# Softmax sums from the exp instruction to VectorE, chains one pair later, token-shift products on ScalarE

## The chip, the cores and the metric

One Trainium2 chip, all 8 of its cores, one launch. Each core works on one half of one of the four sequences and needs nothing from the others while it runs; cores of a pair read the same 4096 tokens in opposite order of halves. The metric is the device time in microseconds (us) of the slowest core, as a median over runs.

## The reference, cut to what matters

```python
x = x + attn(layernorm(x))            # x: (4, 4096, 1024) f32
x = x + ffn(layernorm(x))

def attn(z):                          # Wq, Wk, Wv: 1024 x 64
    q, k, v = z @ Wq, z @ Wk, z @ Wv
    att = softmax(einsum('bid,bkd->bik', q, k), axis=1)   # over the QUERIES i, for each key k
    return tile(att @ v, (1, 1, 16))  # 64 columns, repeated 16 times

def ffn(z):                           # W_r, W_k, W_v: 1024 x 1024
    z_prev = z shifted by one token (zeros first)
    xr = mu_r * z + (1 - mu_r) * z_prev
    xk = mu_k * z + (1 - mu_k) * z_prev
    r = sigmoid(xr @ W_r.T)
    return r * (square(relu(xk @ W_k.T)) @ W_v.T)
```

The softmax normalises each key over all 4096 queries. So with keys on the partitions its sum is one sum per partition over 4096 elements, and 1/sum can be multiplied into the key's row of v.

## The kernel before, in words

Every core normalises all 4096 tokens, computes q, k and v for them, runs the attention of all 4096 keys against all 4096 queries (columns of its own half are kept, see below), and runs the second layernorm and the feed-forward part for its own 2048 tokens. One program is written as a row of blocks per engine; each engine takes its blocks in program order, and counted semaphores tie them: SM counts TensorE's groups, SV VectorE's instructions, SS ScalarE's, the others count DMAs by 16.

The stages, in order:

- **A, layernorm** (L318 to L427): 32 tiles of 128 tokens, written to DRAM as bf16 and brought back transposed as `zT`.
- **C, projections** (L434 to L489): q and k, each written twice (`qrep`, `krep`: the same 64 rows on both halves of the partitions), then v, which goes through DRAM (`vdram`) and comes back as `v_sb` in 32 transposing DMAs, one after the other, on SyncE's queue (L485). TensorE's scores for the first pair wait only for the projections.
- **D, attention** (L515 to L608). Keys come in tiles `kt` of 128, 32 of them, handled as 16 pairs `q` = (2q, 2q+1). For each pair the queries are cut into 4 strips `s` of 1024. TensorE writes the scores of one strip of one key tile into one of three PSUM units of 128x1024 (two matmuls of 512 columns, L544); the even tile uses the upper 64 rows of the array, the odd one the lower 64. A unit is free again when the exp three places back has read it (`d_exp(ktp_, sp_)`, L539). VectorE takes a maximum of every fourth of the first 512 scores of the tile (`reduce_max` to `negm`, L569). ScalarE takes exp of each strip with bias `negm`, writes bf16 into `p_sb[kt % 4]` (4 buffers of 128x4096) and, by `accum_out`, the strip's sum into `ellp` (L604). VectorE then runs what is called **the chain** here, per key tile: add the four strip sums (`ell`, L575), reciprocal (`rell`, L579), scale the tile's 64 columns of v (`vs_sb`, L582), copy one column of p (`xp_sb`, L585). TensorE adds the tile's part of the output, v times p, over four strips of 512 query columns (4 matmuls, L525; they run two at a time, on the two column halves of the array), in `dpool[:, 0:1024]`.
- **E** (L620 to L679): that sum is copied out (L623), turned to token order, and one extra token, the one before the core's half, is treated by a row of tiny steps.
- **F, second layernorm** (L697 to L819), result to DRAM as `z1dram`, and back transposed as `z1T` (8 tiles by 128 channels x 2080 tokens). The first halves of the token range are 8 DMAs issued by ScalarE (L827), the second halves 8 more, each waiting for the one before (L836), issued by ScalarE too.
- **H, token shift** (L855 to L879): per channel tile `ct` VectorE computes `xr[ct]` in two instructions (L864: `z1T * mu`; L867: `z1T shifted * (1 - mu) + that`), in place, and after all eight `xr` the same for `xk` (L873, L876).
- **I, J, K**: r (L897, sigmoid L910), the squared relu (L937, L953, L962), the last product with the sum and the stores (L994, L1039 to L1049). TensorE begins I after the last `xr` (`h_xr_all`); the first sigmoid waits until all of H is done (`SV_H`, L907), as `r_sb` lies where `z1T` was.

What sets the order around the change is the order on each engine in stage D:

- TensorE, pair q (from q = 2): the output matmuls of tiles 2q-4 and 2q-3, each behind `d_vsc` of its tile (the scaled v), and only behind them the 16 score matmuls of pair q.
- VectorE, pair q, before: maximum of 2q, maximum of 2q+1, chain of 2q, chain of 2q+1. A chain waits for the last exp of its tile (`d_exp(kt, 3)`).
- ScalarE, pair q: eight exps, strip by strip, even and odd tile by turns; the first of each tile waits for its maximum, for the row `ell` of two tiles back, and for the output matmuls of four tiles back.

Of the kernel before, what the change touches and what calls it, by code (L numbers as in the profile page):

```python
# [26 lines left out]
def build_program(debug=False):  # L27
# [33 lines left out]
    with ctx:  # L61
# [6 lines left out]
        mu = e(nc.sbuf_tensor("mu", [128, 16], F32))  # L68
# [137 lines left out]
        SM_D0, SS_D0, SV_D0 = SM_C, SS_A, SV_C  # L206
# [9 lines left out]
        def d_outmm(t):  # L216
            q = t // 2
            if q <= 13:
                return SM_D0 + d_P(q + 2) - 4 * (1 - (t % 2))
            return SM_D0 + 368 + 8 * (q - 14) + 4 * (t % 2 + 1)  # L220
        d_exp = lambda kt, s: SS_D0 + 8 * (kt // 2) + 2 * s + (kt % 2) + 1
        d_max = lambda kt: SV_D0 + 10 * (kt // 2) + (kt % 2) + 1
        d_ellsum = lambda kt: SV_D0 + 10 * (kt // 2) + 3 + 4 * (kt % 2)
        d_recip = lambda kt: SV_D0 + 10 * (kt // 2) + 4 + 4 * (kt % 2)
        d_vsc = lambda kt: SV_D0 + 10 * (kt // 2) + 5 + 4 * (kt % 2)
        d_xp = lambda kt: SV_D0 + 10 * (kt // 2) + 6 + 4 * (kt % 2)
        SM_D = SM_D0 + 384
        SS_D = SS_D0 + 128
        SV_D = SV_D0 + 160
        e_evac = SV_D + 2  # L230
        e_tpmm = lambda b: SM_D + b + 1
        e_oxmm = SM_D + 16 + KT
# [2 lines left out]
        SM_E = e_oxmm  # L235
# [31 lines left out]
        F_CNT, SV_Floop = plan_ln_af2(TOWN, SV_TAIL)  # L267
# [3 lines left out]
        SS_F = SS_TAIL + 20  # L271
# [6 lines left out]
        sd_zero2 = SD_E0 + 96  # L278
        SD_F = sd_zero2
        szt_g_hi = lambda ct: 16 * (ct + 1)  # L280
        SV_H0 = SV_F + 1
        h_xr_all = SV_H0 + 16
        SV_H = SV_H0 + 32
        SH_ALL = 0
        SM_I0, SS_I0 = SM_E, SS_F
        i_mm = lambda t: SM_I0 + t + 1
        i_sig = lambda t: SS_I0 + t + 1
        SM_I = SM_I0 + 16
# [272 lines left out]

        @block.vector
        def _(v):
            for q in range(KT // 2):
                for a in range(2):
                    kt = 2 * q + a
                    u0 = d_eidx(kt, 0) % 3
                    v.wait_ge(SM, d_smm(kt, 1))
                    v.reduce_max(negm[:, kt:kt + 1],  # L569
                                 units[u0][:, 0:512:4],  # L570
                                 axis=AX.X, negate=True).then_inc(SV, 1)
                for a in range(2):
                    kt = 2 * q + a
                    v.wait_ge(SS, d_exp(kt, 3))
                    v.reduce_sum(ell[:, kt:kt + 1],  # L575
                                 ellp[:, 4 * (kt % 2):4 * (kt % 2) + 4],
                                 axis=AX.X).then_inc(SV, 1)
                    v.wait_ge(SV, d_ellsum(kt))
                    v.reciprocal(rell[:, kt:kt + 1], ell[:, kt:kt + 1]).then_inc(SV, 1)  # L579
                    v.wait_ge(SV, d_recip(kt))  # L580
                    v.wait_ge(SVT, 16 * (kt + 2))
                    v.tensor_scalar(vs_sb[:, kt * D:(kt + 1) * D],  # L582
                                    v_sb[:, kt * D:(kt + 1) * D],
                                    rell[:, kt:kt + 1], None, ALU.mult).then_inc(SV, 1)
                    v.tensor_copy(xp_sb[:, kt:kt + 1],  # L585
                                  p_sb[kt % 4][:, 4095:4096]).then_inc(SV, 1)

        @block.scalar
        def _(sc):
            for q in range(KT // 2):  # L590
                for s in range(4):
                    for a in range(2):
                        kt = 2 * q + a
                        u = d_eidx(kt, s) % 3
                        if s == 0:
                            if kt == 0:
                                sc.wait_ge(SVT, 16)
                            sc.wait_ge(SV, d_max(kt))
                            if kt >= 2:
                                sc.wait_ge(SV, d_ellsum(kt - 2))  # L600
                            if kt >= 4:
                                sc.wait_ge(SM, d_outmm(kt - 4))
                        sc.wait_ge(SM, d_smm(kt, 2 * s + 1))
                        sc.activation(p_sb[kt % 4][:, s * 1024:(s + 1) * 1024],  # L604
                                      units[u][:, :], AF.Exp,
                                      bias=negm[:, kt:kt + 1],
                                      accum_out=ellp[:, 4 * (kt % 2) + s:
                                                     4 * (kt % 2) + s + 1]).then_inc(SS, 1)  # L608

        @block.gpsimd  # L610
        def _(g):
# [209 lines left out]
        @block.scalar  # L821
        def _(sc):
            sc.wait_ge(SD, sd_zero1)
            for s in range(8):
                sc.wait_ge(ZSs[s], 16)
            for ctn in range(CT):
                sc.dma_start(out=z1T[ctn][:, 0:1040],  # L827
                             in_=z1dram[0:1040, ctn * 128:(ctn + 1) * 128],
                             transpose=True).then_inc(SG_LO, 16)
            sc.wait_ge(SD, sd_zero2)  # L830
            for s in range(8):
                sc.wait_ge(ZSs[s], 32)
            sc.wait_ge(SG_LO, 128)
            for ctn in range(CT):
                sc.wait_ge(SG_HI, 16 * ctn)
                sc.dma_start(out=z1T[ctn][:, 1040:2080],  # L836
                             in_=z1dram[1040:2080, ctn * 128:(ctn + 1) * 128],
                             transpose=True).then_inc(SG_HI, 16)

# [12 lines left out]
        xr = opens(xr_cm)  # L852
        dbuf = zst[:, 0:2048]

        @block.vector  # L855
        def _(v):
            v.wait_ge(SS, f_square(15))
            v.scalar_tensor_tensor(mu1m[:, :], mu[:, :], -1.0, onec[:, :],
                                   ALU.mult, ALU.add).then_inc(SV, 1)
            v.wait_ge(SV, SV_H0)  # L860
            for ct in range(CT):
                v.wait_ge(SG_HI, szt_g_hi(ct))
                v.wait_ge(SV, SV_H0 + 2 * ct)
                v.tensor_scalar(xr[ct][:, :], z1T[ct][:, 16:2064],  # L864
                                mu[:, ct:ct + 1], None, ALU.mult).then_inc(SV, 1)
                v.wait_ge(SV, SV_H0 + 2 * ct + 1)
                v.scalar_tensor_tensor(xr[ct][:, :], z1T[ct][:, 15:2063],  # L867
                                       mu1m[:, ct:ct + 1],
                                       xr[ct][:, :], ALU.mult,
                                       ALU.add).then_inc(SV, 1)  # L870
            for ct in range(CT):
                v.wait_ge(SV, SV_H0 + 16 + 2 * ct)
                v.tensor_scalar(xk[ct][:, :], z1T[ct][:, 16:2064],  # L873
                                mu[:, 8 + ct:9 + ct], None, ALU.mult).then_inc(SV, 1)
                v.wait_ge(SV, SV_H0 + 16 + 2 * ct + 1)
                v.scalar_tensor_tensor(xk[ct][:, :], z1T[ct][:, 15:2063],  # L876
                                       mu1m[:, 8 + ct:9 + ct],
                                       xk[ct][:, :], ALU.mult,
                                       ALU.add).then_inc(SV, 1)  # L879
# [231 lines left out]
```

## Time and profile before

| | us |
|---|---|
| median of 2 runs | 744.12 |
| the two runs | 739.31, 748.92 |
| the profiled execution, its own time | 739.37 |
| span of its slowest core (core 7), from which all rows are | 737.8 |
| spans of the 8 cores | 724.1 to 737.8 |
| VectorE, ScalarE, TensorE matmuls busy | 308.8, 244.0, 364.9 |

The span runs from the first to the last instruction of the core; 1.6 us lie around it. In rows, a time at the start of a line is us from the start of the span, and the number behind it the duration in us (of several instructions, where the line ends in x2 or more, from the first start to the last end or busy together). PE is TensorE (PEld its weight loads), DVE VectorE, ACT ScalarE, POOL GpSimd, SP SyncE; a name with q is that engine's queue of instructions and DMA issues. Square brackets hold the idle time of the engine before the instruction, and what ended it.

### The profile page before, as it was taken

To read this page: it belongs to the slowest core of one execution; us is meant where nothing else is said; L and a number is where in the kernel's file an instruction comes from. 1 tells how busy PE (TensorE), PEld (TensorE's weight loads), DVE (VectorE), ACT (ScalarE), POOL (GpSimd) and SP (SyncE) were. 2 spreads that over 40 slices of the span, in tenths; PEclk is the share of its full clock that TensorE was granted. 3 is DMA by queue.
4 is the path that set the end of the run, shared out by engine and by line. 5 is a ranking of instruction groups with operands and counts; after the bars stand their busy time and mean duration, and the time that the engine had idled before them with its cause. 6 is when DMAs were issued, how large, how long until landed. Compare 5 with 4: busy or idle time off the path is not lost.

```text
span 737.8 us, 5703 instructions; the slowest of 8 cores (724.1 to 737.8 us)
## 1 busy us (share of the span) xinstructions
PE 364.9 (49%) x1392; PEld 125.0 (17%) x1392; DVE 308.8 (42%) x531; ACT 244.0 (33%) x420; POOL 25.4 (3%) x45
## 2 busy tenths in 40 slices
PE   0004000006967888888872000000509999998984
PEld 0001000002421111111111000000104444443431
DVE  4702608147721101111131598808980002226987
ACT  3204013050028898889850233200012233330000
POOL 2000000000000030000000011000000000001110
PEclk9999655556985555555555555555659999999998
DMA  9966985837010099900000045284100000008664
GB/s 237 293 140 81 309 126 190 229 93 161 11 30 8 6 128 160 277 20 0 1 0 1 5 169 172 85 162 78 21 0 0 1 1 1 0 1 274 229 234 175
DMA packets 79044, 75.82 MB, mean 103 GB/s; under 512 B 59427, under 2 KB 59443, under 8 KB 78948
## 3 DMA queue, kind: packets, MB, share of 16 engines
q1 hardware_dynamic: 17124, 38.88, 15.9%
q0 software_dynamic: 10944, 23.93, 14.2%
q10 hardware_dynamic: 50944, 12.65, 10.7%
q8 instruction: 12, 0.20, 0.1%
q14 instruction: 20, 0.16, 0.1%
HBM read 47.79 MB, written 21.56 MB: 94 GB/s over the span
## 4 chain that ended last, share of the span: by engine, by line
DMA 27%; PE 22%; DVE 21%; issue 13%; ACTq 7%; ACT 6%; SPq 2%; DVEq 1%
DMA v_sb<-vdram 10%; PE ktp L937 7%; PE rps L897 7%; ACTq L362 5%; DMA zdram<-zst 5%; DMA z1T<-z1dram 4%; ACT p_sb L604 4%; DMA y_out<-x2b 3%; DVE x1b L735 3%; DMA xst<-x_in 3%; DVE xk L876 3%; PE dpool L544 2%; DVE tmp L1043 2%; DVE sums L415 2%; DVE tmp L1039 2%
## 5 line engine op out<-in xcount | busy, mean ns | idle before, releaser
L604 ACT ACTIVATE p_sb<-dpool,negm 128x1024 bf16<-128x1024 f32 x128 | 140.6, 1125 | 21.9 <-DVE negm L569 21.9
L897 PE MATMUL rps<-wrT,xr 128*128 128x512 bf16 x256 | 59.4, 397 | 150.4 <-DVE xr L867 131.0
L544 PE MATMUL dpool<-qrep,krep 64*128 64x512 bf16 x256 | 110.8, 605 | 32.7 <-ACT p_sb L604 27.3
L443 PE MATMUL qk<-zT,wqk 128*128 128x512 bf16 x64 | 18.5, 441 | 163.6 <-DVE qrep L474 99.1
L348 ACT ACTIVATE zst<-xst 128x1024 bf16<-128x1024 f32 x32 | 33.8, 1056 | 104.2 <-issue 91.7
L994 PE MATMUL ops<-wvT,kaT 128*128 128x512 bf16 x256 | 58.4, 387 | 8.2 <-DVE tmp L1039 6.6
L575 DVE TENSOR_REDUCE ell<-ellp 128x1 f32<-128x4 f32 x32 | 5.0, 157 | 134.7 <-ACT p_sb L604 134.7
L897 PEld LDWEIGHTS rps<-wrT,xr 128*128 128x128 bf16 x256 | 25.8, 101 | 183.6 <-issue 156.1
L937 PE MATMUL ktp<-xk,wkT 128*128 128x512 bf16 x256 | 55.6, 379 | 1.7 <-ACT r_sb L910 1.3
L962 DVE TENSOR_TENSOR kaT<-kaT 128x512 bf16<-128x512 bf16 x32 | 13.6, 425 | 97.6 <-ACT kaT L953 97.5
L415 DVE TENSOR_REDUCE sums<-xst 128x1 f32<-128x1024 f32 x32 | 37.3, 1211 | 11.8 <-DMA xst<-x_in 11.8
L544 PEld LDWEIGHTS dpool<-qrep,krep 64*128 64x128 bf16 x256 | 16.8, 105 | 125.0 <-issue 124.8
L372 DVE TENSOR_SCALAR smean<-sums,cconst 128x4 f32<-128x4 f32 x12 | 2.8, 229 | 81.5 <-ACT zst L348 80.1
L443 PEld LDWEIGHTS qk<-zT,wqk 128*128 128x128 bf16 x64 | 6.8, 108 | 173.0 <-issue 167.4
L994 PEld LDWEIGHTS ops<-wvT,kaT 128*128 128x128 bf16 x256 | 24.9, 99 | 41.7 <-issue 14.5
L953 ACT ACTIVATE kaT<-ktp 128x512 bf16<-128x512 f32 x32 | 19.0, 597 | 34.5 <-PE ktp L937 34.5
L937 PEld LDWEIGHTS ktp<-xk,wkT 128*128 128x128 bf16 x256 | 24.9, 98 | 32.3 <-issue 2.6
L812 ACT ACTIVATE zst<-x1b 128x1024 bf16<-128x1024 f32 x16 | 16.9, 1056 | 36.1 <-DVE x1b L735 36.1
L910 ACT ACTIVATE r_sb<-rps 128x1024 bf16<-128x1024 f32 x16 | 16.3, 1024 | 36.1 <-PE rps L897 36.1
L604 ACT ACTIVATION_READ_ACCUMULATOR p_sb<-dpool,negm 128x1 f32 x128 | 27.7, 217 | 0.0
L525 PE MATMUL dpool<-p_sb,v_sb 128*64 128x512 bf16 x112 | 26.9, 634 | 0.0
L910 ACT ACT_TABLE_LOAD x1 | 1.3, 1283 | 75.5 <-DVE xk L876 75.5
(82 smaller groups left out, 369.5 us busy)
## 6 DMA issues: line engine op xcount, KB each, us to landing
xst<-x_in SPq DMA_DIRECT2D x32, 512.0 KB, 9.0
xst<-x_in POOLq DMA_DIRECT2D x32, 512.0 KB, 6.7
zdram<-zst SPq DMA_DIRECT2D x32, 256.0 KB, 8.2
y_out<-x2b SPq DMA_DIRECT2D x16, 512.0 KB, 3.4
z1dram<-z1b SPq DMA_DIRECT2D x16, 256.0 KB, 2.9
wrT<-wrT_in POOLq DMA_DIRECT2D x1, 2048.0 KB, 19.2
wkT<-wkT_in POOLq DMA_DIRECT2D x1, 2048.0 KB, 31.2
wvT<-wvT_in POOLq DMA_DIRECT2D x1, 2048.0 KB, 44.2
```

Of the source, the lines that this page charges most:

```text
L348: sc.activation(zst[:, (i % 8) * C:(i % 8 + 1) * C], xst[:, (i % 8) * C:(i % 8 + 1) * C], AF.Square, accum_out=sumsq[:, i % 8:i % 8 + 1]). ...
L362: sc.dma_start(out=zT[ctn][:, qtr * 1024:(qtr + 1) * 1024], in_=zdram[qtr * 1024:(qtr + 1) * 1024, ctn * 128:(ctn + 1) * 128], transpose=T ...
L415: v.reduce_sum(sums[:, i % 8:i % 8 + 1], xst[:, (i % 8) * C:(i % 8 + 1) * C], axis=AX.X).then_inc(SV, 1)
L443: t.matmul(qk[buf][:, :], wqk[:, ct * 128:(ct + 1) * 128], zT[ct][:, nch * 512:(nch + 1) * 512], start=(ct == 0), stop=(ct == CT - 1), ski ...
L525: t.matmul(dpool[64 * half:64 * half + 64, (w % 2) * 512:(w % 2) * 512 + 512], vs_sb[:, tt_ * D:(tt_ + 1) * D], p_sb[tt_ % 4][:, w * 512:( ...
L544: t.matmul(units[u][:, cc * 512:(cc + 1) * 512], krep[64 * a:64 * (a + 1), kt * 128:(kt + 1) * 128], qrep[64 * a:64 * (a + 1), c * 512:(c ...
L604: sc.activation(p_sb[kt % 4][:, s * 1024:(s + 1) * 1024], units[u][:, :], AF.Exp, bias=negm[:, kt:kt + 1], accum_out=ellp[:, 4 * (kt % 2) + s:
L735: v.tensor_tensor(x1b[:, s8 * C:(s8 + 1) * C], xst[:, s8 * C:(s8 + 1) * C], bass.AP(out_tok, t_ * D, [[TOWN * D, 128], [0, 16], [1, D]]), ...
L876: v.scalar_tensor_tensor(xk[ct][:, :], z1T[ct][:, 15:2063], mu1m[:, 8 + ct:9 + ct], xk[ct][:, :], ALU.mult, ALU.add).then_inc(SV, 1)
L897: ins = t.matmul(r_ps[t_ % 2][:, hh * 512:(hh + 1) * 512], xr[ct][:, t_ * 128:(t_ + 1) * 128], wrT[:, ct * C + hh * 512:ct * C + (hh + 1) ...
L937: ins = t.matmul(kt_ps[ix % 2][:, :], wkT[:, ct * C + dt * 128:ct * C + (dt + 1) * 128], xk[ct][:, tc * 512:(tc + 1) * 512], start=(ct == ...
L994: ins = t.matmul(o_ps[t_ % 2][:, hh * 512:(hh + 1) * 512], kaT[dt][:, t_ * 128:(t_ + 1) * 128], wvT[:, dt * C + hh * 512:dt * C + (hh + 1) ...
```

## The change

Three parts.

1. **Softmax sums.** The exp (L604) has no `accum_out` any more. VectorE's `reduce_sum` in the chain reads the four strips themselves, 128x4096 bf16 of `p_sb[kt % 4]`, in place of the four numbers of `ellp`. ScalarE's wait for `ell` of two tiles back goes; for kt >= 4 a wait comes for `d_xp(kt - 4)`, the last instruction of the chain that reads the same buffer of p.
2. **Order on VectorE.** In pair q the two maxima come first, and then the chains of pair q-1, not of q; the chains of pair 15 follow at the end. TensorE's order is as it was.
3. **Token shift.** The two products `z1T * mu` of each channel tile go from VectorE to ScalarE (`Identity` with a scale per partition). VectorE keeps the second instruction of each. The 8 second-half transposes of `z1T` go from ScalarE's queue to SyncE's, with the same waits.

```diff
-        d_max = lambda kt: SV_D0 + 10 * (kt // 2) + (kt % 2) + 1
...
+        D_CNT = {}
+        _sv = SV_D0
+        for _q in range(16):
+            for _a in range(2):
+                _sv += 1
+                D_CNT[("max", 2 * _q + _a)] = _sv
+            if _q >= 1:
+                for _a in range(2):
+                    _kt = 2 * (_q - 1) + _a
+                    for _op in ("ellsum", "recip", "vsc", "xp"):
+                        _sv += 1
+                        D_CNT[(_op, _kt)] = _sv
...
         @block.vector
         def _(v):
+            def d_chain(v, kt):
+                v.wait_ge(SS, d_exp(kt, 3))
+                v.reduce_sum(ell[:, kt:kt + 1],
+                             p_sb[kt % 4][:, :],
+                             axis=AX.X).then_inc(SV, 1)
+                v.wait_ge(SV, d_ellsum(kt))
+                v.reciprocal(rell[:, kt:kt + 1], ell[:, kt:kt + 1]).then_inc(SV, 1)
+                v.wait_ge(SV, d_recip(kt))
+                v.wait_ge(SVT, 16 * (kt + 2))
+                v.tensor_scalar(vs_sb[:, kt * D:(kt + 1) * D],
+                                v_sb[:, kt * D:(kt + 1) * D],
+                                rell[:, kt:kt + 1], None, ALU.mult).then_inc(SV, 1)
+                v.tensor_copy(xp_sb[:, kt:kt + 1],
+                              p_sb[kt % 4][:, 4095:4096]).then_inc(SV, 1)
...
-                for a in range(2):
-                    kt = 2 * q + a
-                    v.wait_ge(SS, d_exp(kt, 3))
-                    v.reduce_sum(ell[:, kt:kt + 1],
-                                 ellp[:, 4 * (kt % 2):4 * (kt % 2) + 4],
-                                 axis=AX.X).then_inc(SV, 1)
...
+                if q >= 1:
+                    for a in range(2):
+                        d_chain(v, 2 * (q - 1) + a)
+            for a in range(2):
+                d_chain(v, 30 + a)
...
-                            if kt >= 2:
-                                sc.wait_ge(SV, d_ellsum(kt - 2))
                             if kt >= 4:
+                                sc.wait_ge(SV, d_xp(kt - 4))
                                 sc.wait_ge(SM, d_outmm(kt - 4))
...
-                                      bias=negm[:, kt:kt + 1],
-                                      accum_out=ellp[:, 4 * (kt % 2) + s:
-                                                     4 * (kt % 2) + s + 1]).then_inc(SS, 1)
+                                      bias=negm[:, kt:kt + 1]).then_inc(SS, 1)
...
-            sc.wait_ge(SD, sd_zero2)
+        @block.sync
+        def _(sy):
+            sy.wait_ge(SD, sd_zero2)
             for s in range(8):
-                sc.wait_ge(ZSs[s], 32)
-            sc.wait_ge(SG_LO, 128)
+                sy.wait_ge(ZSs[s], 32)
+            sy.wait_ge(SG_LO, 128)
             for ctn in range(CT):
-                sc.wait_ge(SG_HI, 16 * ctn)
-                sc.dma_start(out=z1T[ctn][:, 1040:2080],
+                sy.wait_ge(SG_HI, 16 * ctn)
+                sy.dma_start(out=z1T[ctn][:, 1040:2080],
...
+        @block.scalar
+        def _(sc):
+            sc.wait_ge(SV, F_CNT[("apply", 15)])
+            for ct in range(CT):
+                sc.wait_ge(SG_HI, szt_g_hi(ct))
+                sc.activation(xr[ct][:, :], z1T[ct][:, 16:2064], AF.Identity,
+                              bias=0.0, scale=mu[:, ct:ct + 1]).then_inc(SS, 1)
+            for ct in range(CT):
+                sc.activation(xk[ct][:, :], z1T[ct][:, 16:2064], AF.Identity,
+                              bias=0.0, scale=mu[:, 8 + ct:9 + ct]).then_inc(SS, 1)
...
             for ct in range(CT):
-                v.wait_ge(SG_HI, szt_g_hi(ct))
-                v.wait_ge(SV, SV_H0 + 2 * ct)
-                v.tensor_scalar(xr[ct][:, :], z1T[ct][:, 16:2064],
-                                mu[:, ct:ct + 1], None, ALU.mult).then_inc(SV, 1)
-                v.wait_ge(SV, SV_H0 + 2 * ct + 1)
+                v.wait_ge(SS, h_tsr(ct))
+                v.wait_ge(SV, SV_H0 + ct)
                 v.scalar_tensor_tensor(xr[ct][:, :], z1T[ct][:, 15:2063],
...
```

The semaphore counts of later stages follow (`SS_H` 16 more on ScalarE, `SV_H` 16 fewer on VectorE).

## Rows read from the trace of the kernel before

**Rows 1.** Busy by stretch: TensorE, weight loads, VectorE, ScalarE, GpSimd; granted clock, DMA share, GB/s
```profile
175.00:215.00 40.00, 36.23 (x162) 15.62 (x160) 22.91 (x35) 0.00 (x0) 0.00 (x0) 0.96 0.32 59
...
250.00:420.00 170.00, 118.03 (x362) 24.91 (x360) 32.77 (x159) 116.38 (x210) 6.89 (x11) 0.51 0.34 64
```

**Rows 2.** Timeline, one pair of key tiles in steady state, and its successor's first exp
```profile
337.55 1.92 PE L525 MATMUL dpool<-p_sb,v_sb 128*64 128x512 bf16 x8
...
339.40 1.88 PE L544 MATMUL dpool<-qrep,krep 64*128 64x512 bf16 x6
...
339.86 0.16 DVE L575 TENSOR_REDUCE ell<-ellp 128x1 f32<-128x4 f32 x1 [0.20 <-ACT p_sb L604]
...
340.46 0.24 DVE L582 TENSOR_SCALAR v_sb<-v_sb,rell 128x64 bf16<-128x64 bf16 x1 [0.18 <-DVE rell L579]
...
340.68 0.48 DVE L569 TENSOR_REDUCE negm<-dpool 128x1 f32<-128x128 f32 x2
341.22 1.11 ACT L604 ACTIVATE p_sb<-dpool,negm 128x1024 bf16<-128x1024 f32 x1 [1.47 <-DVE negm L569]
342.23 0.19 ACT L604 ACTIVATION_READ_ACCUMULATOR p_sb<-dpool,negm 128x1 f32 x1
342.33 1.11 ACT L604 ACTIVATE p_sb<-dpool,negm 128x1024 bf16<-128x1024 f32 x1
...
351.56 1.11 ACT L604 ACTIVATE p_sb<-dpool,negm 128x1024 bf16<-128x1024 f32 x1 [1.47 <-DVE negm L569]
```

**Rows 3.** Groups by line and shape: busy us, mean ns; idle before, releasers
```profile
L415 DVE TENSOR_REDUCE sums<-xst 128x1 f32<-128x1024 f32 x32 | 37.3, 1211 | 11.8 <-DMA xst<-x_in 11.8
...
L604 ACT ACTIVATION_READ_ACCUMULATOR p_sb<-dpool,negm 128x1 f32 x128 | 27.7, 217 | 0.0
...
L735 DVE TENSOR_TENSOR x1b<-xst,out_tok 128x1024 f32<-128x1024 f32 x16 | 19.4, 1213 | 0.0
...
L962 DVE TENSOR_TENSOR kaT<-kaT 128x512 bf16<-128x512 bf16 x32 | 13.6, 425 | 97.6 <-ACT kaT L953 97.5
...
L575 DVE TENSOR_REDUCE ell<-ellp 128x1 f32<-128x4 f32 x32 | 5.0, 157 | 134.7 <-ACT p_sb L604 134.7
```

**Rows 4.** Timeline, the last chain and the output matmuls behind it
```profile
381.83 0.24 DVE L582 TENSOR_SCALAR v_sb<-v_sb,rell 128x64 bf16<-128x64 bf16 x1 [0.18 <-DVE rell L579]
...
382.30 0.22 PEld L554 LDWEIGHTS dpool<-p_sb,v_sb 128*64 128x64 bf16 x4 [0.88 <-issue]
383.33 1.22 DVE L623 COPY out_sb<-dpool 64x1024 f32<-64x1024 f32 x1 [1.20 <-PE dpool L554]
```

**Rows 5.** Timeline, the first pair: scores, maxima, first exp
```profile
211.51 1.02 PE L544 MATMUL dpool<-qrep,krep 64*128 64x512 bf16 x6 [0.94 <-DVE p_sb L478]
212.21 0.49 DVE L569 TENSOR_REDUCE negm<-dpool 128x1 f32<-128x128 f32 x2 [0.84 <-PE dpool L544]
...
217.16 1.11 ACT L604 ACTIVATE p_sb<-dpool,negm 128x1024 bf16<-128x1024 f32 x1
```

**Rows 6.** Timeline, token shift: last two xr instructions, first and last xk, what follows
```profile
521.36 0.75 DVE L864 TENSOR_SCALAR xr<-z1T,mu 128x2048 bf16<-128x2048 bf16 x1 [0.39 <-DMA z1T<-z1dram]
522.22 2.35 DVE L867 SCALAR_TENSOR_TENSOR xr<-z1T,mu1m,xr 128x2048 bf16<-128x2048 bf16 x1
524.68 0.75 DVE L873 TENSOR_SCALAR xk<-z1T,mu 128x2048 bf16<-128x2048 bf16 x1
...
548.75 2.35 DVE L876 SCALAR_TENSOR_TENSOR xk<-z1T,mu1m,xk 128x2048 bf16<-128x2048 bf16 x1
551.24 1.28 ACT L910 ACT_TABLE_LOAD   x1 [75.47 <-DVE xk L876]
```

**Rows 7.** Groups of ScalarE by shape, for the price of a 2048-element product
```profile
L953 ACT ACTIVATE kaT<-ktp 128x512 bf16<-128x512 f32 x32 | 19.0, 597 | 34.5 <-PE ktp L937 34.5
...
L812 ACT ACTIVATE zst<-x1b 128x1024 bf16<-128x1024 f32 x16 | 16.9, 1056 | 36.1 <-DVE x1b L735 36.1
L910 ACT ACTIVATE r_sb<-rps 128x1024 bf16<-128x1024 f32 x16 | 16.3, 1024 | 36.1 <-PE rps L897 36.1
```

More of the change, by code:

```diff
@@ L221, in build_program @@
         d_exp = lambda kt, s: SS_D0 + 8 * (kt // 2) + 2 * s + (kt % 2) + 1
-        d_max = lambda kt: SV_D0 + 10 * (kt // 2) + (kt % 2) + 1
[L223 to L226, printed above, removed]
+        D_CNT = {}
[10 more added lines that the diff above has]
+                        D_CNT[(_op, _kt)] = _sv
+        for _a in range(2):
+            _kt = 30 + _a
+            for _op in ("ellsum", "recip", "vsc", "xp"):
+                _sv += 1
+                D_CNT[(_op, _kt)] = _sv
+        d_max = lambda kt: D_CNT[("max", kt)]
+        d_ellsum = lambda kt: D_CNT[("ellsum", kt)]
+        d_recip = lambda kt: D_CNT[("recip", kt)]
+        d_vsc = lambda kt: D_CNT[("vsc", kt)]
+        d_xp = lambda kt: D_CNT[("xp", kt)]
         SM_D = SM_D0 + 384
         SS_D = SS_D0 + 128
-        SV_D = SV_D0 + 160
+        SV_D = _sv
+        assert SV_D == SV_D0 + 160
         e_evac = SV_D + 2
@@ L280, in build_program @@
         szt_g_hi = lambda ct: 16 * (ct + 1)
+        SS_H0 = SS_F
+        h_tsr = lambda ct: SS_H0 + ct + 1
+        h_tsk = lambda ct: SS_H0 + 8 + ct + 1
+        SS_H = SS_H0 + 16
         SV_H0 = SV_F + 1
-        h_xr_all = SV_H0 + 16
-        SV_H = SV_H0 + 32
+        h_xr_all = SV_H0 + 8
+        SV_H = SV_H0 + 16
         SH_ALL = 0
-        SM_I0, SS_I0 = SM_E, SS_F
+        SM_I0, SS_I0 = SM_E, SS_H
         i_mm = lambda t: SM_I0 + t + 1
@@ L571, in _ @@
                                  axis=AX.X, negate=True).then_inc(SV, 1)
-                for a in range(2):
-                    kt = 2 * q + a
-                    v.wait_ge(SS, d_exp(kt, 3))
-                    v.reduce_sum(ell[:, kt:kt + 1],
-                                 ellp[:, 4 * (kt % 2):4 * (kt % 2) + 4],
-                                 axis=AX.X).then_inc(SV, 1)
[L578 to L586, printed above, removed]
+                if q >= 1:
[3 more added lines that the diff above has]
+                d_chain(v, 30 + a)
         @block.scalar
@@ L871, in _ @@
             for ct in range(CT):
[L872 to L875, printed above, removed]
+                v.wait_ge(SS, h_tsk(ct))
+                v.wait_ge(SV, SV_H0 + 8 + ct)
                 v.scalar_tensor_tensor(xk[ct][:, :], z1T[ct][:, 15:2063],
```

## The prediction

> **What bounds the kernel now.** I read the stretches first (busy time by stage), then the chain of waits, then the timeline of each place that the change touches, and last the groups of instructions by shape for prices. The stage that matters is the attention. From 250 to 420 us ScalarE is busy 116 of 170 us, VectorE 33, TensorE 118 at a granted clock of 0.51, its lower level of 1.2 GHz [rows 1]. One pair of key tiles takes 351.56 - 341.22 = 10.34 us [rows 2]: eight exps that start 1.09 to 1.11 us apart (8.8 us), and some 1.5 us in which ScalarE waits for the maximum of the next pair, which VectorE takes only after both chains of this pair. So ScalarE's exps set the pair, with a short turn over VectorE in between; VectorE is free for most of it. Sixteen pairs, from the first exp at 217.16 [rows 5] to the copy of the result at 383.33 [rows 4], are 166.2 us. The second place is the token shift, where VectorE works alone: its products and sums end at 548.75 + 2.35 = 551.1, and the first sigmoid's table load starts at 551.24 [rows 6]. TensorE stands still behind it.
>
> **Part 1: the exp without its sum.** The 128 accumulator reads cost 27.7 us of busy time [rows 3], but they overlap their neighbours: the read starts 1.01 us after its exp, and the next exp 0.10 us after the read [rows 2]. Without the read the next instruction can start at the same 1.01, so an exp saves 0.1 us, a pair 0.8 us: 8.1 us of exps. That would be about 13 us in all, if ScalarE still set the pair.
>
> **Part 2: the sum on VectorE.** The four-element sum (0.157 us, 32 times [rows 3]) becomes one over 4096 bf16. The trace has no such instruction. The same operation takes 1211 ns for 1024 elements and 157 for 4 [rows 3]: (1211 - 157) / 1020 = 1.033 ns an element, and 157 + 4092 x 1.033 = 4.39 us. Those inputs are f32. The other end: an elementwise bf16 operation takes 425 ns for 512, where an f32 one takes 1213 for 1024 [rows 3], so some bf16 work goes at twice the rate; a sum at that rate would take 157 + 4092 x 0.517 = 2.27 us. On the other hand `scalar_tensor_tensor` on bf16 needs 2.35 us for 2048 [rows 6], 1.15 ns an element, so bf16 alone speeds nothing up; at its rate the sum takes 4.71. I take 4.39, from the same operation, and keep 2.27 and 4.71 as ends.
>
> The Trainium skill has a rule for just this: VectorE: DVE Perf Modes, section "The perf-mode tier table", says that `tensor_reduce` has a program for one element a cycle only, in bf16 as in f32, while tensor_tensor goes twice as fast in bf16. No row of the kernel before shows a bf16 sum, so the trace neither confirms nor denies it. By this rule the sum stays at 4.39, by the tensor_tensor row it would be 2.27. The rule speaks against the change.
>
> **The chain.** In rows 2 the second chain starts its sum at 339.86; take off the sum's 0.16. From the sum's end to the end of the scaled v (340.46 + 0.24) is 0.68 us, to the start of the next VectorE instruction (340.68) 0.66. So a chain now takes 4.39 + 0.66 = 5.05 us, and 4.39 + 0.68 = 5.07 to its scaled v. Two of them are 10.1 us, against 8.1 us of exps: VectorE is the slower engine.
>
> **The order, and the loop that it closes.** The chains of pair q-1 now follow the maxima of pair q. TensorE was not reordered: before its scores for pair q it must do the output matmuls of tile 2q-3, which need that tile's scaled v. Before, that v was ready a pair earlier. Now it is made by VectorE directly ahead of the maximum of 2q. That maximum needs the scores of pair q, they stand in TensorE's queue behind those output matmuls, and these need the chain just ended. VectorE cannot run ahead, since its own next instruction is that maximum. So each pair goes round one closed loop:
>
> - from the scaled v of 2q-3 to the weight load of its output matmuls 0.23 us (381.83 + 0.24 = 382.07 to 382.30 [rows 4]);
> - 0.03 to the matmuls, and half of the 339.40 - 337.55 = 1.85 us that eight of them hold TensorE [rows 2]: 0.93;
> - the first two score matmuls, until VectorE starts its maximum. At a granted clock of 0.96 [rows 1] this was 212.21 - 211.51 = 0.70 us [rows 5]. Two 512-column matmuls are 0.43 us of it at 2.4 GHz and 0.86 at 1.2 GHz, where the attention runs: 1.13;
> - the second maximum waits for two more score matmuls. Six take 1.88 us [rows 2], so two take 0.63 where they overlap; then its own 0.24 (two are 0.48 [rows 2]);
> - the two chains of pair q-1, whose exps are long done: 5.05 + 5.07.
>
> The sum is 0.23 + 0.03 + 0.93 + 1.13 + 0.63 + 0.24 + 10.12 = 13.3 us a pair, against 10.34. ScalarE starts pair q's exps after the maxima, needs 8.1 us and then waits some 5 us. The new wait for `d_xp(kt - 4)` costs nothing, as the maximum of the same tile is later on VectorE; the saved 0.1 us per exp is worth nothing, as it lies in that wait.
>
> **The attention from end to end.** The first exp stays at 217.16. The sixth ends at 217.16 + 5 x 1.01 + 1.11 = 223.3, which frees the unit for the first scores of pair 1. The second unit comes free 1.0 later (224.3), and with 1.2 us for scores and signalling the second maximum starts at 225.5 and ends at 225.8. There the first sum starts. Fourteen rounds later (14 x 13.3 = 186.3) the chain of tile 28 starts, at 412.1; three chains and a last scaled v (3 x 5.05 + 5.07 = 20.2) end at 432.3, and the copy of the result follows 383.33 - 382.07 = 1.26 us later [rows 4]: 433.6. Against 383.33 that is **+50.3 us**. The transposes of v and the load of the three big weights lie beside this stretch as before and get more cover.
>
> **Part 3: the token shift.** The transposes arrive one by one, since each waits for the one before; that stays. I put their pace on SyncE's queue at the same value: SyncE has stored the last of `z1dram` by then, and has nothing else until the output stage. ScalarE's product of 2048 elements: 597 ns for 512 and 1024 for 1024 [rows 7] give 427 per 512; 1056 for 1024 out of SBUF [rows 7] and twice 427 more make 1.91; a per-partition operand adds up to 0.09 (exp 1.11 against sigmoid 1.02 [rows 2, 7]): 2.0 us. For `xr` the arrival sets the pace, and only the last counts: the last product starts at 521.36 as before, but takes 2.0 in place of the 0.86 to 522.22 [rows 6]. The last `xr` ends 1.1 us later, at about 525.7 in place of 524.6. For `xk` ScalarE keeps ahead (1.9 us apiece against VectorE's 2.46, from 522.22 to 524.68 [rows 6]), so VectorE has eight times 2.46: 525.8 + 7 x 2.46 + 2.35 = 545.4 in place of 551.1. That is **-5.7 us** on the path, since the sigmoids, and behind them TensorE, wait for all of it. TensorE's first two tiles (9 us) end well before either way.
>
> **Sum**: 739.4 of the profiled execution + 50.3 - 5.7 = **784.0 us**. That execution is 4.8 us under the median of two, equal to the lower of them; I go by it.
>
> **Rivals.**
>
> *The sum runs at two bf16 elements a cycle* (2.27 us). For it: the 425 ns row. Against it: every reduction in the trace fits one line through a full cycle an element, and the page's rule. The loop is then 3.2 for the hand-over and twice 2.94, 9.1 us a pair; the maxima of pair 15 end near 225.8 + 14 x 9.1 = 353, the exp of tile 30 ends near 360, its chain and that of tile 31 (2 x 2.94) near 366, and the copy starts near 367. That is -16, with the token shift -22: **718 us**, faster. It decides below 2.9 us a sum: there a pair costs as much as before: 3.2 + 2 x (2.9 + 0.67) = 10.3. Chance 0.08.
>
> *VectorE is the bound, but TensorE's part of the loop hides* (the wait for the scaled v met early, as where the queue of TensorE had room). Then a pair is 2 x 5.05 + 0.5 = 10.6 us, the sixteen pairs end at 225.8 + 14 x 10.6 + 20.2 + 1.3 = 396, +12.4, and with the token shift +6.7: **746 us**, no change that can be told. For it: VectorE's busy time alone says so. Against it: the order of waits in the code. Chance 0.04.
>
> *The sum is slower still* (4.71 us, or ScalarE's writes and VectorE's reads of p get in each other's way): 30 sums on the path at 0.32 each, 794 us. It is within the forecast's own range. *TensorE gets the upper clock, since its work now comes in other portions*: that takes 0.9 us from each round (0.43 from the scores, half of the 0.93), -13, 771 us. The granted clock was 0.51 all through this stage while TensorE was busier than it will be, so I expect none of it. *The moved transposes cost more from SyncE's queue*: half a us each would be 4 us, and also within it.
>
> **Numbers.** Forecast 0.88, the fast sum 0.08, the hidden loop 0.04. Within the forecast the ends are 770 (the upper clock, or both maxima back to back and shorter waits) and 803 (4.71 us, a disturbed median as in the higher run before). Both other cases are left out, 0.12. Faster by over 2% 0.08, within 2% 0.05, slower by over 2% 0.87; 2% (15 us) is about what can be told from no change here.
>
> **What would show it.** In the changed profile: the bf16 sum at 4.4 us x32, VectorE's busy time up by 32 x 4.2 = 135 us; pairs of exps 13.3 us apart, with one idle stretch of some 5 us on ScalarE each, released by the maximum; TensorE idle before its output matmuls, released by the scaled v; VectorE idle some 2 us before its first maximum of a pair, released by TensorE. Exps 1.01 us apart. In the token shift the `xk` sums 2.46 us apart. Wrong it is if the sum takes 2.3 us, or if the maximum starts less than 1 us after the scaled v.

## The result, and the profile after

| | before | after |
|---|---|---|
| median us (runs) | 738.65 (10) | 778.78 (11) |
| ratio | | 1.0553, 95% interval 1.0525 to 1.0581 |
| profiled execution, us | 739.37 | 773.85 |
| span of its slowest core, us | 737.8 (core 7) | 772.3 (core 3) |

The kernel became slower by 40 us in the medians, 34.5 in the profiled executions. The medians are over all runs; ratios and intervals, here and below, leave out the few runs in a slower state of the chip (789.5 us after, for one), which is why 778.78 / 738.65 is a little less than 1.0553. The page after, busy time first and then the groups that the change touched (busy us, mean ns; idle before them and who ended it):

```profile
PE 367.3 (48%) x1392; PEld 123.3 (16%) x1392; DVE 431.6 (56%) x515; ACT 264.7 (34%) x309; POOL 25.4 (3%) x45
...
DVE ell L588 17%; PE ktp L969 7%; PE rps L929 7%; ACTq L384 5%; DMA zdram<-zst 4%; DMA z1T<-z1dram 4%; DMA y_out<-x2b 3%; DMA xst<-x_in 3%; DVE x1b L759 2%; DVE xk L908 2%; PE dpool L547 2%; PE dpool L566 2%; DMA v_sb<-vdram 2%; ACTq L851 2%; DVE sums L437 2%
...
L630 ACT ACTIVATE p_sb<-dpool,negm 128x1024 bf16<-128x1024 f32 x128 | 130.3, 1134 | 68.6 <-DVE negm L606 63.5
L588 DVE TENSOR_REDUCE ell<-p_sb 128x1 f32<-128x4096 bf16 x32 | 141.1, 4408 | 0.0
...
L547 PE MATMUL dpool<-p_sb,v_sb 128*64 128x512 bf16 x112 | 29.9, 630 | 42.7 <-DVE xp_sb L598 42.7
...
L606 DVE TENSOR_REDUCE negm<-dpool 128x1 f32<-128x128 f32 x32 | 7.9, 287 | 46.4 <-PE dpool L566 46.4
```

Three idle times name the ring: ScalarE waited 63.5 us for maxima, VectorE's maxima 46.4 us for TensorE's scores, TensorE's output matmuls 42.7 us for the end of a chain (the profile names its last instruction, the copy to `xp_sb`, beside which the scaled v came ready). The bf16 sum took 4408 ns, and it leads the chain of waits at 17% of the span. VectorE is busy 122.8 us more than before (431.6 against 308.8): 136.1 more in the sums (141.1 against 5.0 [rows 3]), less 12.0 in the 16 products that went to ScalarE.

One round of the loop, from the timeline after (start us, us; the weight loads of TensorE are left out but for one):

```profile
337.85 0.24 DVE L595 TENSOR_SCALAR v_sb<-v_sb,rell 128x64 bf16<-128x64 bf16 x1 [0.18 <-DVE rell L592]
...
338.31 0.22 PEld L547 LDWEIGHTS dpool<-p_sb,v_sb 128*64 128x64 bf16 x4 [3.83 <-issue]
338.34 1.07 PE L547 MATMUL dpool<-p_sb,v_sb 128*64 128x512 bf16 x4 [2.98 <-DVE xp_sb L598]
...
339.34 1.89 PE L566 MATMUL dpool<-qrep,krep 64*128 64x512 bf16 x6
...
340.48 0.49 DVE L606 TENSOR_REDUCE negm<-dpool 128x1 f32<-128x128 f32 x2 [2.33 <-PE dpool L566]
340.89 4.41 DVE L588 TENSOR_REDUCE ell<-p_sb 128x1 f32<-128x4096 bf16 x1
341.04 8.15 ACT L630 ACTIVATE p_sb<-dpool,negm 128x1024 bf16<-128x1024 f32 x8 [4.81 <-DVE negm L606]
...
345.95 4.41 DVE L588 TENSOR_REDUCE ell<-p_sb 128x1 f32<-128x4096 bf16 x1
...
350.81 0.24 DVE L595 TENSOR_SCALAR v_sb<-v_sb,rell 128x64 bf16<-128x64 bf16 x1 [0.17 <-DVE rell L592]
...
353.48 0.49 DVE L606 TENSOR_REDUCE negm<-dpool 128x1 f32<-128x128 f32 x2 [2.37 <-PE dpool L566]
```

Read it as a ring: scaled v (ends 338.09), output matmuls (338.34), scores (339.34), maxima (340.48), two sums (340.89, 345.95), the next scaled v (ends 351.05), and the next maxima at 353.48: 13.00 us a pair, against 10.34 before [rows 2]. ScalarE did its eight exps in 8.15 us and was idle 4.81. From the first exp (215.42) to the copy of the result (427.72) the attention took 212.3 us, against 166.2: **+46.1 us**. On the other seven cores it was 212.8 after, and on those of the kernel before 165.9 to 166.4. TensorE's granted clock over this stretch was 0.50, as before.

The token shift: first the issue of the second-half transposes before, then the stretch of [rows 6] after:

```profile
493.16 25.66 ACTq L836 DMA_TRANSPOSE z1T<-z1dram  x8
```

```profile
533.83 25.48 SPq L862 DMA_TRANSPOSE z1T<-z1dram  x8
...
561.56 2.00 ACT L886 ACTIVATE xr<-z1T,mu 128x2048 bf16<-128x2048 bf16 x1 [1.36 <-DMA z1T<-z1dram]
...
563.73 2.35 DVE L901 SCALAR_TENSOR_TENSOR xr<-z1T,mu1m,xr 128x2048 bf16<-128x2048 bf16 x1 [1.01 <-ACT xr L886]
566.19 19.54 DVE L908 SCALAR_TENSOR_TENSOR xk<-z1T,mu1m,xk 128x2048 bf16<-128x2048 bf16 x8
...
585.86 1.28 ACT L942 ACT_TABLE_LOAD   x1 [7.16 <-DVE xk L908]
```

From the issue of the first second-half transpose to the sigmoid's table load it is 52.03 us; before it was 58.08 (493.16 to 551.24 [rows 6]): **-6.0 us**. Together that is +40.1 us, which is also the difference of the medians. The profiled spans differ by 34.5 only, and the -5.6 us that are left lie in neither place. 1.7 of it lies ahead of the first exp (215.42 against 217.16). 4.2 of it is one step of stage E: from the store of the extra token's 64 numbers to the first instruction that uses them core 7 before needed 16.4 us and core 3 after 12.2; the eight cores lie between 13.8 and 16.4 before, between 12.2 and 16.6 after. The two ranges overlap, so I take it for scatter between cores and no work of the change.

### The profile page after: what moved, and what is told of

The parts are those of the page before. It is cut to its first block, busy times and chain, and to the rows that moved or that the text cites. A ratio compares the mean times of both kernels' runs of the same rounds, so it can differ in the third digit from the quotient of the medians.

```text
span 772.3 us, 5575 instructions; the slowest of 8 cores (765.5 to 772.3 us)
## 1 busy us (share of the span) xinstructions
PE 367.3 (48%) x1392; PEld 123.3 (16%) x1392; DVE 431.6 (56%) x515; ACT 264.7 (34%) x309; POOL 25.4 (3%) x45
## 3 DMA queue, kind: packets, MB, share of 16 engines
q0 software_dynamic: 10944, 23.93, 13.3%
## 4 chain that ended last, share of the span: by engine, by line
DVE 38%; PE 23%; DMA 18%; issue 9%; ACTq 7%; ACT 3%; SPq 2%; DVEq 1%
DVE ell L588 17%; PE ktp L969 7%; PE rps L929 7%; ACTq L384 5%; DMA zdram<-zst 4%; DMA z1T<-z1dram 4%; DMA y_out<-x2b 3%; DMA xst<-x_in 3%; DVE x1b L759 2%; DVE xk L908 2%; PE dpool L547 2%; PE dpool L566 2%; DMA v_sb<-vdram 2%; ACTq L851 2%; DVE sums L437 2%
## 5 line engine op out<-in xcount | busy, mean ns | idle before, releaser
L630 ACT ACTIVATE p_sb<-dpool,negm 128x1024 bf16<-128x1024 f32 x128 | 130.3, 1134 | 68.6 <-DVE negm L606 63.5
L588 DVE TENSOR_REDUCE ell<-p_sb 128x1 f32<-128x4096 bf16 x32 | 141.1, 4408 | 0.0
L566 PE MATMUL dpool<-qrep,krep 64*128 64x512 bf16 x256 | 109.2, 605 | 23.7 <-ACT p_sb L630 22.7
L465 PE MATMUL qk<-zT,wqk 128*128 128x512 bf16 x64 | 18.4, 439 | 162.6 <-DVE qrep L496 99.0
L547 PE MATMUL dpool<-p_sb,v_sb 128*64 128x512 bf16 x112 | 29.9, 630 | 42.7 <-DVE xp_sb L598 42.7
L465 PEld LDWEIGHTS qk<-zT,wqk 128*128 128x128 bf16 x64 | 6.8, 108 | 172.0 <-issue 166.4
L901 DVE SCALAR_TENSOR_TENSOR xr<-z1T,mu1m,xr 128x2048 bf16<-128x2048 bf16 x8 | 18.8, 2351 | 27.5 <-ACT xr L886 27.4
L606 DVE TENSOR_REDUCE negm<-dpool 128x1 f32<-128x128 f32 x32 | 7.9, 287 | 46.4 <-PE dpool L566 46.4
L985 ACT ACTIVATE kaT<-ktp 128x512 bf16<-128x512 f32 x32 | 19.0, 597 | 34.5 <-PE ktp L969 34.5
## 6 DMA issues: line engine op xcount, KB each, us to landing
wrT<-wrT_in POOLq DMA_DIRECT2D x1, 2048.0 KB, 17.9
```

The lines of the kernel that those rows point to most:

```text
L465: t.matmul(qk[buf][:, :], wqk[:, ct * 128:(ct + 1) * 128], zT[ct][:, nch * 512:(nch + 1) * 512], start=(ct == 0), stop=(ct == CT - 1), ski ...
L547: t.matmul(dpool[64 * half:64 * half + 64, (w % 2) * 512:(w % 2) * 512 + 512], vs_sb[:, tt_ * D:(tt_ + 1) * D], p_sb[tt_ % 4][:, w * 512:( ...
L566: t.matmul(units[u][:, cc * 512:(cc + 1) * 512], krep[64 * a:64 * (a + 1), kt * 128:(kt + 1) * 128], qrep[64 * a:64 * (a + 1), c * 512:(c ...
L588: v.reduce_sum(ell[:, kt:kt + 1], p_sb[kt % 4][:, :], axis=AX.X).then_inc(SV, 1)
L630: sc.activation(p_sb[kt % 4][:, s * 1024:(s + 1) * 1024], units[u][:, :], AF.Exp, bias=negm[:, kt:kt + 1]).then_inc(SS, 1)
L985: sc.activation(kaT[dt][:, tc * 512:(tc + 1) * 512], kt_ps[ix % 2][:, :], AF.Relu).then_inc(SS, 1)
```

## The experiments

Each ratio is to runs of the kernel before that were made beside it: median 732.94 for the first four experiments, 737.94 for the last three. Expectations in us were built on the 739 of the result, so a difference to before says more than a time. "The attention" is always first exp to copy of the result.

**scores_first.** The changed kernel, with TensorE's first strip of scores ahead of the output matmuls (and the counts of SM to match):

```diff
             for q in range(KT // 2):
-                if q >= 2:
-                    for tt_ in (2 * (q - 2), 2 * (q - 2) + 1):
...
                 for s in range(4):
+                    if s == 1 and q >= 2:
+                        for tt_ in (2 * (q - 2), 2 * (q - 2) + 1):
...
                     for a in range(2):
```

> The changed kernel with one edit: TensorE writes the first strip of scores of pair q (both tiles) ahead of the output matmuls of tiles 2q-4 and 2q-3. Theory (closed loop over the scaled v): the 2.9 us between the copy of a chain and the next first sum shrink to the two maxima, 0.5 us, so a pair takes 2 x 5.07 + 0.5 = 10.6 us in place of 13.0 and the attention 8.6 + 14 x 10.6 + 21.8 = 179 us in place of 212: about 745 us. Rival (the sums on VectorE, or TensorE's own work, set the pair whatever the order): 13.0 us a pair and 778 us.

Measured 738.64, 1.0079 of before (1.0051 to 1.0108): 34 us of the 40 are gone by an edit that adds and removes no instruction. Its timeline, VectorE and TensorE round the maxima:

```profile
332.45 8.18 ACT L630 ACTIVATE p_sb<-dpool,negm 128x1024 bf16<-128x1024 f32 x8 [2.37 <-DVE negm L606]
...
342.57 0.15 DVE L598 COPY xp_sb<-p_sb 128x1 bf16<-128x1 bf16 x1
342.63 0.48 DVE L606 TENSOR_REDUCE negm<-dpool 128x1 f32<-128x128 f32 x2
342.91 1.07 PE L548 MATMUL dpool<-p_sb,v_sb 128*64 128x512 bf16 x4 [1.13 <-DVE negm L606]
343.02 4.41 DVE L588 TENSOR_REDUCE ell<-p_sb 128x1 f32<-128x4096 bf16 x1
343.17 8.16 ACT L630 ACTIVATE p_sb<-dpool,negm 128x1024 bf16<-128x1024 f32 x8 [2.54 <-DVE negm L606]
```

The maxima follow the copy at once and carry no idle time: the scores were ready. This pair took 343.17 - 332.45 = 10.72 us; most others took 10.53, and the attention 178.3, where 179 was expected. So the order of TensorE's queue closed the loop. What is left of it, 12 us over the attention before, is VectorE at full load (busy 94.3 us of the 100 from 250 to 350): two chains and two maxima. The token shift gives 6 of the 12 back.

**sum_only.** The kernel before with part 1 alone, ScalarE's new wait for `d_xp(kt - 4)` with it; the chains stay behind the maxima of their own pair:

```diff
-                                 ellp[:, 4 * (kt % 2):4 * (kt % 2) + 4],
+                                 p_sb[kt % 4][:, :],
...
-                                      accum_out=ellp[:, 4 * (kt % 2) + s:
-                                                     4 * (kt % 2) + s + 1]).then_inc(SS, 1)
+                                      bias=negm[:, kt:kt + 1]).then_inc(SS, 1)
```

> The kernel before with part 1 alone: the sum over p on VectorE, the chains directly behind the maxima of their own pair. Theory: a pair is 0.6 us to the first exp, 7.1 us to the last exp of the even tile, two chains of 5.07 and the next maxima: 17.9 us a pair in place of 10.3, so 121 us more, about 860. Rival (the chains of pair q overlap the exps of pair q+1, as VectorE is not needed by them): at most 13 us a pair, 780.

Measured 852.73, one run and so no interval: 120 over before, against 121 expected. The attention was 288 us, 122 over before.

```profile
335.23 0.48 DVE L569 TENSOR_REDUCE negm<-dpool 128x1 f32<-128x128 f32 x2
335.77 8.14 ACT L603 ACTIVATE p_sb<-dpool,negm 128x1024 bf16<-128x1024 f32 x8 [9.79 <-DVE negm L569]
...
343.01 4.42 DVE L575 TENSOR_REDUCE ell<-p_sb 128x1 f32<-128x4096 bf16 x1 [7.31 <-ACT p_sb L603]
...
348.09 4.41 DVE L575 TENSOR_REDUCE ell<-p_sb 128x1 f32<-128x4096 bf16 x1
```

ScalarE and VectorE work by turns: 9.79 us idle on the one, 7.31 on the other, in this pair. Most pairs took 17.93 us, and 17.9 were expected. So part 2 of the change is what part 1 needs: in the attention it takes 122 us of loss down to 46.

**order_only.** The kernel before with part 2 alone (the chains of pair q-1 behind the maxima of pair q, as in the change's diff), the exp keeping its sum, in 16 places of `ellp` (written by `accum_out` and read by the sum; the cut shows the read):

```diff
-                                 ellp[:, 4 * (kt % 2):4 * (kt % 2) + 4],
+                             ellp[:, 4 * (kt % 4):4 * (kt % 4) + 4],
...
-                            if kt >= 2:
-                                sc.wait_ge(SV, d_ellsum(kt - 2))
                             if kt >= 4:
+                                sc.wait_ge(SV, d_xp(kt - 4))
```

> The kernel before with part 2 alone: the exp keeps its sum (16 places of ellp in place of 8), and the chains of pair q-1 follow the maxima of pair q. Theory: the chains are short (0.8 us each) and off the path, but the maximum of pair q waits behind the output matmuls of pair q-2 (1.9 us on TensorE), which start only after the last scores of pair q-1. I expect a stall of about 1.3 us a pair in place of 1.5, so 10.0 us a pair and 4 us less in all: about 735. Rival (the turn over VectorE between pairs is the whole stall, and it goes with the order): 8.8 us a pair, 24 us less: about 715.

Measured 730.88, 0.9958 (0.9922 to 0.9994), 2 us less by the medians and 3 by the ratio; a pair took 345.39 - 335.18 = 10.21 us, the attention 162.6, which is 3.6 less. The timeline, where one pair meets the next:

```profile
335.18 1.11 ACT L626 ACTIVATE p_sb<-dpool,negm 128x1024 bf16<-128x1024 f32 x1 [1.34 <-DVE ell L584]
...
341.85 1.92 PE L543 MATMUL dpool<-p_sb,v_sb 128*64 128x512 bf16 x8
...
343.70 1.73 PE L562 MATMUL dpool<-qrep,krep 64*128 64x512 bf16 x6
...
344.84 0.49 DVE L602 TENSOR_REDUCE negm<-dpool 128x1 f32<-128x128 f32 x2 [7.93 <-PE dpool L562]
...
345.39 1.11 ACT L626 ACTIVATE p_sb<-dpool,negm 128x1024 bf16<-128x1024 f32 x1 [1.34 <-DVE ell L584]
```

VectorE has been idle for 7.93 us when the maximum comes, so it is not late; the scores are, since 1.9 us of output matmuls stand ahead of them.

**shift_only.** The kernel before with part 3 as it stands in the change's diff (both edits of ScalarE, SyncE and VectorE), and no other.

> The kernel before with part 3 alone (products on ScalarE, second-half transposes issued by SyncE). Theory: 8 xk sums 2.46 us apart in place of 3.32, less 0.9 us at the last xr: 6 us less, 0.992 of before. Rival (the moved transposes or the extra table load give it back): within 1 us of before.

Measured 727.06, 0.9916 (0.9886 to 0.9946): 6 us less, as expected. The `xk` sums stand as one block, and the table load behind it is released by it:

```profile
515.95 19.54 DVE L888 SCALAR_TENSOR_TENSOR xk<-z1T,mu1m,xk 128x2048 bf16<-128x2048 bf16 x8
...
535.62 1.28 ACT L922 ACT_TABLE_LOAD   x1 [7.16 <-DVE xk L888]
```

19.54 us for eight, 2.46 apart, as in the changed kernel.

**half_sum.** The changed kernel with the sum over half of p:

```diff
-                             p_sb[kt % 4][:, :],
+                             p_sb[kt % 4][:, 0:2048],
```

> The changed kernel with the sum taken over the first 2048 of the 4096 elements of p only, so half of each softmax sum is left out. Theory (loop): a sum of 2048 costs 157 + 2044 x 1.039 = 2.28 us, the loop is 2.9 + 2 x 2.94 = 8.8 us a pair, just over the 8.2 to 8.7 that ScalarE and its restart need, and the attention about 146 us: 712 in all, faster than before. This is also what a sum at two elements a cycle would have given. Rival (something else than the sum's length holds the pair near 10 us, such as TensorE at its lower clock): 730 or more.

Measured 724.23 (two runs), 0.9813 (0.9757 to 0.9869). Faster than before, as the theory says, but 12 us over its number. First the sum's group, then the timeline:

```profile
L588 DVE TENSOR_REDUCE ell<-p_sb 128x1 f32<-128x2048 bf16 x32 | 72.8, 2276 | 1.4 <-ACT p_sb L630 1.4
```

```profile
330.62 8.14 ACT L630 ACTIVATE p_sb<-dpool,negm 128x1024 bf16<-128x1024 f32 x8 [1.62 <-DVE negm L606]
...
336.47 0.15 DVE L598 COPY xp_sb<-p_sb 128x1 bf16<-128x1 bf16 x1
336.84 1.92 PE L547 MATMUL dpool<-p_sb,v_sb 128*64 128x512 bf16 x8
338.69 1.88 PE L566 MATMUL dpool<-qrep,krep 64*128 64x512 bf16 x6
339.83 0.49 DVE L606 TENSOR_REDUCE negm<-dpool 128x1 f32<-128x128 f32 x2 [3.22 <-PE dpool L566]
340.24 2.28 DVE L588 TENSOR_REDUCE ell<-p_sb 128x1 f32<-128x2048 bf16 x1
340.38 8.14 ACT L630 ACTIVATE p_sb<-dpool,negm 128x1024 bf16<-128x1024 f32 x8 [1.61 <-DVE negm L606]
```

The sum had its price (2276 ns, 2.28 expected). But a pair took 340.38 - 330.62 = 9.76 us here in place of 8.8, and the attention 159.3 in place of 146: the chain was done at 336.6, and all eight output matmuls (336.84, behind the last scores of the pair) stood between it and the maxima at 339.83. The loop over the scaled v had given way to the stall of order_only, which the expectation left out. The rival was right that something else than the sum holds the pair near 10 us.

**order_shift_sf.** Parts 2 and 3 of the change, the exp keeping its sum in 16 places of `ellp`, and TensorE's order of scores_first (edits as above).

> Parts 2 and 3, the exp keeping its sum (as in order_only), and TensorE writing the first strip of scores of a pair ahead of the output matmuls. Theory: the maximum no longer waits for output matmuls; the 1.9 us of them now delay the second strip by 0.5 us, so 9.25 us a pair, 16 us less than before, and 6 from the token shift: about 711, 0.970 of before. Rival (the stall at the pair's start is not from the place of the output matmuls): as order_only with the shift, 723.

Measured 727.97, 0.9868 (0.9819 to 0.9918), 10 us less and not 22: the theory failed, and the rival's number came, though not by its reason. A pair took hardly less than in order_only (346.36 - 336.22 = 10.14 us against 10.21). Why stands in the last row:

```profile
336.22 1.11 ACT L630 ACTIVATE p_sb<-dpool,negm 128x1024 bf16<-128x1024 f32 x1 [1.27 <-PE dpool L548]
...
344.16 0.29 DVE L606 TENSOR_REDUCE negm<-dpool 128x1 f32<-128x128 f32 x1 [6.95 <-PE dpool L566]
...
345.07 1.92 PE L548 MATMUL dpool<-p_sb,v_sb 128*64 128x512 bf16 x8
...
346.36 1.11 ACT L630 ACTIVATE p_sb<-dpool,negm 128x1024 bf16<-128x1024 f32 x1 [1.27 <-PE dpool L548]
```

The maximum is there at 344.45, and ScalarE still starts at 346.36, released by the output matmuls: it writes into the buffer of p that these read (four tiles back). The scores had been moved off that wait, and the buffer put another one in its place.

**order_spread.** The same, with the output matmuls of pair q-1 inside pair q, so a pair earlier:

```diff
-                    if s == 1 and q >= 2:
-                        for tt_ in (2 * (q - 2), 2 * (q - 2) + 1):
+                    if s >= 2 and q >= 1:
+                        for tt_ in (2 * (q - 1) + s - 2,):
...
-            for tt_ in range(KT - 4, KT):
+            for tt_ in range(KT - 2, KT):
```

> As order_shift_sf, but the output matmuls of pair q-1 stand in pair q, four ahead of the third strip of scores and four ahead of the fourth. Theory: ScalarE's eight exps of 1.09 us are the pair, 8.75 us, and TensorE at 1.2 GHz just keeps up (16 x 0.43 and 1.9 us): 8.8 to 9.0 us a pair, 22 us less than before, and 6 from the token shift: about 705, 0.962 of before. Rival (TensorE at its lower clock is the bound, as output and score matmuls don't overlap): 9.3 us a pair or more, 712.

Measured 711.36, **0.9635 (0.9594 to 0.9675)**: the fastest of all kernels here, 27 us under before, where the theory had 28. (In us it lies at the rival's 712; the pair tells the two apart.) First ScalarE's group, then the timeline from one pair to the next:

```profile
L631 ACT ACTIVATE p_sb<-dpool,negm 128x1024 bf16<-128x1024 f32 x128 | 140.6, 1124 | 0.5
```

```profile
338.59 1.07 PE L549 MATMUL dpool<-p_sb,v_sb 128*64 128x512 bf16 x4
338.63 1.11 ACT L631 ACTIVATE p_sb<-dpool,negm 128x1024 bf16<-128x1024 f32 x1
...
342.20 0.29 DVE L607 TENSOR_REDUCE negm<-dpool 128x1 f32<-128x128 f32 x1 [5.91 <-PE dpool L567]
...
347.54 1.11 ACT L631 ACTIVATE p_sb<-dpool,negm 128x1024 bf16<-128x1024 f32 x1
```

8.91 us a pair, in the range that was expected, and ScalarE idle 0.5 us in the whole attention, where it had 21.9 before its exps in the kernel before (the page before, the group of its 128 exps). Here the exps are nearly the whole stage: eight times 1.09 is 8.73. The other 0.17 is one exp a pair, the first on the third strip, that starts 1.26 us after the one before it (338.63 after 337.37); its scores stand behind output matmuls. In the first pair, which has no output matmuls, all eight are 1.09 to 1.11 apart.

## Why the prediction was right, point by point

**The sum on VectorE**: 4.39 us taken, 4.408 measured. The line through the f32 sums held for bf16, and 4408 ns against 2276 for half the elements (half_sum) gives the slope once more: 1.04 ns an element, where the f32 sums gave 1.03. The rule of the Trainium skill (VectorE: DVE Perf Modes, section "The perf-mode tier table"), that a `tensor_reduce` goes at one element a cycle in bf16 as in f32, is borne out by these traces: the two slopes are the same.

**The loop**: 13.3 us taken, 13.00 measured, and shown to be a loop by scores_first. Its terms, in order: weight load 0.23 taken and 0.22 measured (338.09 to 338.31); output matmuls 0.96 and 1.03 (to 339.34); scores to the first maximum 1.13 and 1.14; second maximum and its end 0.87 and 0.41; two chains 10.12 and, from the sum at 340.89 to the end of the next scaled v (350.81 + 0.24), 10.16. The measured terms add up to 12.96, which six of the last thirteen rounds took; some longer ones make the mean 13.00. The one term that was mis-sized is **the wait for the second maximum, put at 0.63 us: it was none**. Both maxima stand back to back (0.49 us for two, 0.41 from the first to the sum). The 0.63 was a third of the 1.88 us that six score matmuls take [rows 2], as if they came evenly. They don't: the trace has two of them start at 339.34 and 339.35, two at 339.74 and 339.75, so these run side by side, and the last two start one by one. The view of the first four alone:

```profile
339.34 1.04 PE L566 MATMUL dpool<-qrep,krep 64*128 64x512 bf16 x4
```

The scores of both tiles are there at nearly the same time. [rows 5] could have told: the first pair's two maxima take 0.49 us there too. So this term was 0.46 us too long; the other terms and the longer rounds were 0.15 too short. Over 14 rounds the 0.31 that are left (13.31 - 13.00) make 4.3 us, and 50.3 - 46.1 = 4.2 is what the attention came out short.

**The rest of stage D**: first sum 8.6 us after the first exp, taken and measured (215.42 to 224.03). The first exp itself did not stay at 217.16 but came at 215.42; no part of the change lies ahead of it, and its place cancels in the attention's length. The exps start 1.0 us apart without the read, as taken from [rows 2], and the gain was worth nothing behind a wait of 4.8 us. The wait for `d_xp(kt - 4)` showed nowhere.

**The token shift**: -5.7 taken, -6.0 measured in the profiled executions and about 6 us in shift_only. The product took 2.00 us as taken. The transposes ran at the same pace from SyncE's queue (eight issues in 25.48 us; 25.66 from ScalarE's, in the timeline before), and the last `xr` ended 32.25 us after their start in place of 31.41, 0.8 later where I had 1.1.

**The total**: 784.0 forecast, 773.85 for the profiled execution and 778.78 for the median. The mis-sized term and the -5.6 us that the section on the result puts down to scatter between cores account for the difference to the profiled execution: 784.0 - 4.2 - 0.3 - 5.6 = 773.9. Against the median the scatter plays no part: 784.0, less 0.7 for a base that was above the median of before, less 4.2 and 0.3, is 778.8. That it meets 778.78 so closely is luck, as single runs differ by some us; that it is within the range is not, as each term was measured.

**The rivals.** A sum at two elements a cycle: no, by 4408 ns. The number given for it, 718 or 22 us less, would have been too low: half_sum, which has that sum's price, came out 14 us under before, since at 9.1 us a pair the stall behind the output matmuls (order_only) already decides; its loop was priced alone. The hidden loop, 746 us: it did not happen in the changed kernel, but scores_first is that kernel with room made in TensorE's queue, and it took 10.53 us in most pairs where the rival had 10.6. The upper clock: no, the granted clock was 0.50 over the whole attention. Dearer transposes from SyncE's queue: no, by the pace above.

## What to carry to other kernels

When a chain of one tile is put off by a round on one engine, look at the queue of every engine that it feeds: if the consumer's work is still ahead of the next round's first step, a ring closes, and each round pays all of it in turn. Price a removed instruction by how much nearer its neighbours can start, not by its busy time: 128 accumulator reads with 27.7 us of busy time were worth 0.1 us each (exps 1.00 us apart in place of 1.09), and what replaced them cost 4.4 us a tile. And after a move, name what waits next: here the buffer of p (order_shift_sf) took over from the scores, and the gain came only when the output matmuls went a whole pair earlier.

## What the hardware showed that I had not expected

- The scores of the even and the odd tile, on the two row halves of the array, come ready almost together at 1.2 GHz: both maxima run back to back from 1.14 us after the first score matmul starts, although two matmuls of 512 columns stand before the first and four before the second. The four start two by two, 0.40 us apart.
- `Identity` on ScalarE began with a table load of 1.28 us, at 537.44 in the changed kernel's timeline, before the first product at 538.73. The first product was late by it; the transposes set the pace of the rest, and no row shows it in the time.
- ScalarE's exps alone can set the attention's time: with the stall between pairs gone the first and the last exp lie 141.2 us apart in order_spread (141.1 to 141.3 over the cores), against 162.7 on core 7 before. These 21.5 us are about the idle time that went (21.9 on the page before, 0.5 here).
- TensorE's granted clock in the attention was not the same for all kernels: 0.50 before, after and in scores_first (250 to 350 us), 0.59 in order_spread, 0.67 in order_only (250 to 360 us). The pair times did not follow it. In order_spread the pair from 289.57 to 298.47 ran at 0.50, that is at 1.2 GHz throughout, and took 8.90 us like the others; so TensorE kept up at its lower clock, but for the 0.17 us a pair above.
